# Attention products that name 64 of 128 rows: maxima and scores in a four-layer kernel

## The reference

```python
def _L1_xattn_ref(query, key, values, mask, W_out):      # 16 heads of 16 features, 154 keys
    q = query.reshape(N, Q, HEADS, HEAD_DIM)
    k = key.reshape(N, K, HEADS, HEAD_DIM)
    v = values.reshape(N, K, HEADS, HEAD_DIM)
    energy = jnp.einsum('nqhd,nkhd->nhqk', q, k)
    energy = jnp.where(mask == 0, jnp.float32(-1e+20), energy)
    attn = jax.nn.softmax(energy / jnp.sqrt(jnp.float32(EMB)), axis=-1)
    out = jnp.einsum('nhqk,nkhd->nqhd', attn, v).reshape(N, Q, EMB)
    return out @ W_out.T
x = x + _L1_xattn_ref(_layernorm(x, axis=-1), ctx_1024, ctx_1024, mask_Bx1x1xS2_ik0, L1_xattn_W_out)
```

## Time and profile before

| | |
|---|---|
| median of 3 runs | 815.07 us (814.76 to 815.62) |
| span of the profiled execution | 814.1 us |
| TensorE products busy | 690.2 us, 85% of the span |
| VectorE busy | 632.6 us, 78% |
| ScalarE busy | 486.0 us, 60% |
| attention on TensorE | from about 288 to 545 us |

### The profile page before, as it was taken

How to read it: one execution, slowest core, us unless ns; L and a number is a source line. 1 busy time by engine, 2 the same in 40 slices (tenths; PEclk the granted TensorE clock), 3 DMA queues, 4 the chain that set the end, 5 groups by cost and what they waited for, 6 DMA issues and landing times.

```text
span 814.1 us, 11786 instructions
## 1 busy us (share of the span) xinstructions
PE 690.2 (85%) x4152; PEld 529.5 (65%) x4152; DVE 632.6 (78%) x1244; ACT 486.0 (60%) x621; POOL 313.7 (39%) x249
## 2 busy tenths in 40 slices
PE   6882029999999888999999999999999999009998
PEld 5761026899888754566566656577887888007998
DVE  5988894887777388887767675987888899997654
ACT  2223012554454437796896886666655999796873
POOL 4353604377677735234422420003440444693000
PEclk9995558999999999999999999999999999658999
DMA  9927523456644570010013000003310743201343
GB/s 299 339 81 257 200 80 110 127 137 146 178 88 58 108 254 1 1 47 27 1 47 130 1 27 27 27 27 133 127 52 1 261 152 131 76 0 53 125 135 104
DMA packets 59540, 84.95 MB, mean 104 GB/s; under 512 B 7904, under 2 KB 47712, under 8 KB 57952
## 3 DMA queue, kind: packets, MB, share of 16 engines
q1 hardware_dynamic: 49936, 61.09, 22.3%
q0 software_dynamic: 7872, 21.11, 10.5%
q10 hardware_dynamic: 1680, 2.08, 0.8%
HBM read 53.73 MB, written 30.54 MB: 104 GB/s over the span
## 4 chain that ended last, share of the span: by engine, by line
PE 63%; DVE 14%; ACT 7%; issue 4%; POOL 3%; DMA 1%; POOLq 0%; DVEq 0%; ACTq 0%
PE bank L2101 13%; PE bank L2363 11%; PE bank L2157 8%; PE bank L2387 5%; PE bank L1448 3%; PE bank L1482 3%; PE bank L1505 3%; PE bank L1542 3%; PE bank L1502 3%; DVE above L783 2%; PE bank L1463 2%; PE bank L1486 2%; ACT wgateT L2050 1%; DVE qx L1179 1%; ACT qT L1331 1%
## 5 line engine op out<-in xcount | busy, mean ns | idle before, releaser
L1305 ACT ACTIVATE x<-bank,bic 128x512 f32<-128x512 f32 x160 | 106.2, 697 | 34.1 <-PE bank L1482 32.6
L1179 DVE TENSOR_REDUCE qx<-bank 128x4 fp32r<-128x616 f32 x128 | 98.2, 796 | 27.0 <-PE bank L1448 25.6
L2101 PE MATMUL bank<-ux,uwh 128*128 128x512 f32 x384 | 96.6, 393 | 0.2 <-ACT ux L1995 0.2
L2101 PEld LDWEIGHTS bank<-ux,uwh 128*128 128x128 f32 x384 | 72.5, 189 | 16.0 <-issue 0.6
L1482 PE MATMUL bank<-qT,K 128*128 128x512 f32 x128 | 61.5, 490 | 3.5 <-ACT x L1305 2.0
L2324 ACT ACTIVATE wgateT<-bank 128x512 f32<-128x512 f32 x32 | 19.2, 599 | 65.7 <-PE bank L2363 65.7
L1448 PE MATMUL bank<-Kb,qTb 128*128 128x308 bf16 x256 | 53.2, 298 | 4.9 <-DVE qx L1179 2.2
L2101 PE MATMUL bank<-ux,uwl 128*128 128x512 f32 x192 | 52.0, 393 | 0.0
L1106 POOL CAST qx<-q 128x1024 fp32r<-128x1024 f32 x8 | 8.5, 1068 | 112.7 <-PE bank L1463 104.0
L2363 PE MATMUL bank<-xh,wh 128*128 128x512 f32 x128 | 50.0, 390 | 0.3 <-DVE xl L2297 0.3
L2363 PE MATMUL bank<-xl,wh 128*128 128x512 f32 x128 | 50.0, 390 | 0.0
(11 more groups left out here) (420 smaller groups left out, 2029.0 us busy)
## 6 DMA issues: line engine op xcount, KB each, us to landing
xs_dram<-ux POOLq DMA_DIRECT2D x6, 1024.0 KB, 4.2
ux<-xs_dram POOLq DMA_DIRECT2D x6, 1024.0 KB, 5.3
x_dram<-x SPq DMA_DIRECT2D x4, 1024.0 KB, 5.5
xr<-in_w1T SPq DMA_DIRECT2D x8, 512.0 KB, 3.8
xr<-in_w3T SPq DMA_DIRECT2D x8, 512.0 KB, 4.7
xr<-in_w2T SPq DMA_DIRECT2D x8, 512.0 KB, 6.5
row_dram<-xn SPq DMA_DIRECT2D x8, 512.0 KB, 3.1
x_dram<-xr SPq DMA_DIRECT2D x8, 512.0 KB, 2.9
```

The source lines that it names most:

```text
L1179: dve.tensor_reduce(qx[:, k, g * GH:(g + 1) * GH, MROW].rearrange("p (u h) -> p u h", u=2), pair[i][:].rearrange("p (u x) -> p u x", u=2)[ ...
L1305: act.activation(pr[g % 2][h], S_[u % 2], ACT.Exp, bias=bic[:, s // 2, h // GH:h // GH + 1]).then_inc(p_done, 1)
L2101: mm = pe.matmul(bank[j][:, m * TB:(m + 1) * TB], w[:, c * HI + cols:c * HI + cols + P], x[:, part, c * TB:(c + 1) * TB], start=(w is uwh ...
```

## The change

Both products name the 64 rows that hold something, in the stationary and in the moving operand alike. In `maximum`, u = 0 takes rows 0 to 63 and u = 1 rows 64 to 127. In `score`, heads of even number take rows 0 to 63 and odd ones rows 64 to 127. Nothing else is changed: order, waits, buffers and the work of other engines are the same, and the rows left out were products with zeros.

```diff
                     for u in range(2):
-                        mm = pe.matmul(dst[:, u * QN:u * QN + 2 * S2], qTb[:, k, g, :],
-                                       Kb[s // 2 % 2][:, g, u * 2:u * 2 + 2, :].rearrange("p h s -> p (h s)"), start=True, stop=True)
+                        rows = slice(u * 2 * MW, (u + 1) * 2 * MW)
+                        mm = pe.matmul(dst[:, u * QN:u * QN + 2 * S2], qTb[rows, k, g, :],
+                                       Kb[s // 2 % 2][rows, g, u * 2:u * 2 + 2, :].rearrange("p h s -> p (h s)"), start=True, stop=True)
                     mm.then_inc(sent, 1)
...
                     if h < GH:
                         at = g * GH + h
-                        mm = pe.matmul(dst, K[b % 2][:, at // 2, at % 2, :], qT[s % 2][:, at // 2, :, :].rearrange("p k t -> p (k t)"),
+                        rows = slice(at % 2 * SW, (at % 2 + 1) * SW)
+                        mm = pe.matmul(dst, K[b % 2][rows, at // 2, at % 2, :], qT[s % 2][rows, at // 2, :, :].rearrange("p k t -> p (k t)"),
                                        start=True, stop=True)
```

## The result

The changed kernel takes 830.81 us (828.56 to 831.87, 4 runs) where the kernel before took 814.99 us: +15.8 us, ratio 1.0182 with a 95% interval of 1.0147 to 1.0216. A second series gave 829.37 us and 1.0169 (1.0149 to 1.0189). The forecast was 824.0 us, 810 to 840. The profiled execution of after has a span of 826.8 us against 814.1, +12.7 us, and it is the fastest of the four. Its own time is 828.56 us, 1.8 us above its span, and not 1.0 as I took from the median of before. The runs of the kernel before on record have the same 1.8 us between the two. So its profiled execution was about 0.9 us slower than its median and that of after 2.2 us faster than its own; these two make up the difference between +12.7 and +15.8.

A forecast was written before the change was run, and what follows sets the result against it. TensorE was taken to bound attention's middle. Middle +8.0, first stretch 0 and last +2.8 us, less 2 for further waits, gave +9 us: 823 us on the profiled execution, 824.0 as median, range 810 to 840.

The forecast's parts named there:

- What bounds: Attention's middle, 345 to 510 us: TensorE bounds it, its products busy 163.26 of 165.00 us.
- The gain of a pair: Two products of a maximum run at once, saving 0.13 us a pair, at most 16.6 us in all.
- The sign that I named: In the changed kernel, a pair of maxima's piece of the chain would be near 0.13 us.
- The price of a change: Each new switch of row height costs 0.11 us ahead of a maximum, mostly 0.20 us elsewhere; 25 a steady step.
- What hides: Idle time right ahead of changes in the middle cuts their 24 us to 19.3, leaving +8.0 us after the gain.
- the 2 us taken off: Over all steps, waits not right ahead of a change take up another 2 us of the loss.
- The last stretch: Attention's end: 20 changes at 0.20 us make 4.0 us, of which 2.8 us are left after waits.
- The first stretch, put at 0: Attention's start: changes less gain make +2.7 us, taken as 0 because engines wait for each other.
- The clock rival: Half-height products count for less and TensorE's clock falls to 1.2 GHz for a while: 834 us and above, chance 0.04.
- The median: Whole kernel: the median time stands 1.0 us above the profiled span, turning 823 into 824.0 us.

The follow-up runs named there:

- mx_same: Against mx_only, both products of a pair of maxima take rows 0 to 63, so they can't run at once: 835.69 us, ratio 1.0240.
- probe64: Kernel before plus an unused product of 64 rows and 8 columns ahead of each score: 838.89 us; the same with 128 rows as control: 820.92 us.
- mx_only: Changed kernel with the edit in `score` undone, so only the maxima name 64 rows: 823.53 us, ratio 1.0107.
- score_only: Changed kernel with the edit in `maximum` undone, so only the scores name 64 rows: 839.93 us, ratio 1.0297.
- after_again: The changed kernel run once more with no edit, for its first stretch: 829.37 us, ratio 1.0169.
- after_warm: Changed kernel plus one unused product of 128 rows and 512 columns ahead of each maximum of the second step: 828.57 us, ratio 1.0168.
- same_rows: Changed kernel with both products of each maximum on rows 0 to 63, scores still half-height: 833.34 us, ratio 1.0209.
- dummies64: Kernel before with only the unused products at its start and in the first step named over 64 rows: 829.63 us, ratio 1.0155.

## Why the prediction was right, step by step

- **What bounds.** TensorE in the middle: right, 163 of 165 us before and after.
- **The gain of a pair, 0.13 us.** Right in size: mx_same gives 0.10 net of waits. The sign that I named, a piece of the chain of 0.13 us, was wrong: the piece is 0.24 and the score's 0.22, which together are the 0.46 us from the pair's start to the next product, the wait behind the score included. The starts show the concurrency, the pieces of the chain don't.
- **The price of a change, 0.11 and 0.20 us, taken over from columns and one product over one row.** Right in size. probe64 gives 0.08 us for each change ahead of a short product or behind one, mx_only 0.11 and score_only 0.13, all net of waits; the chain shows +0.20 on L1507 and +0.19 on L1488. Most of it falls on the neighbours of the half-height products, as counted.
- **What hides.** The middle was forecast at 8.0 us in 5.7 steps, 1.4 us a step, before the 2 us taken off; measured 1.19 us a step. Right, a little too high.
- **The last stretch.** From 492.9 us the forecast has 2.8 us and 0.8 us for the rest of the middle, 3.6 together; measured 2.28.
- **The first stretch, put at 0.** This term was mis-sized. At the first mark, 377.59, the forecast has 1.6 us (1.13 steps of the middle); measured 5.57. From attention's own start it is 6.30. The clock has a part in it: it was low for a quarter of that stretch in the profile (column 0.88). As an estimate, if all 13.7 us of low clock cost as much as the 6.9 by which after and after_again differ (1.78 us), the clock took some 3.5 us and the changes of the first steps some 2.8. I had counted 2.7 us of changes there and let the waits take all of them. How the 6.30 us really divide isn't settled; after_warm, with the clock at 1.00, has 5.15 of them left, but 16 products more on the way.
- **Luck.** In span the change cost 12.7 us where 9 were forecast, a miss of 3.7 us, and it would have been larger had the parts not missed in opposite ways: the first mark was 4.0 us later than forecast, the four steps behind it were 0.8 us cheaper (4.77 for 5.6) and the rest 1.3 us cheaper (2.28 for 3.6), while the 2 us taken off for waits were not there.
- **The clock rival.** I gave it a chance of 0.04, as an alternative to the forecast, at 834 us and above. It came true beside the forecast, in spells, and only in the first stretch, where TensorE has waits. In the middle, at 163 of 165 us busy, the clock stayed at 1.00.
- **The median.** +15.8 us against +12.7 us in the profiled spans: the profiled execution is the shortest of four (spans of the others 828.7 to 830.1 us). Over the eight runs of the changed kernel on record the clock, as the mean of the whole execution, goes with the span: the lowest (0.921, twice) has 830.1 and 830.7 us, the highest (0.934) 826.2. But 0.928 stands beside both 826.8 and 829.3, so it explains a part only.

## What to carry to other kernels

Naming only the rows that hold something can pay where half-height products stand next to each other; each switch between heights cost 0.08 to 0.13 us here, in the drain and in a weight load that was hidden before. Count the switches in the order of issue first, price one from a place in the trace where the shape changes, and keep zeros in the idle rows where neighbours are full-height: that was the faster form here. Unused products held the clock here when they were full-height and lost it when they were half-height.

## What the runs showed of the hardware

- Two products of 64 rows in different halves and banks run at once, also a bf16 maximum beside a fp32 score (starts 0.01 us apart in same_rows).
- A change of rows between 64 and 128 costs 0.08 us net of waits in probe64 (0.10 at the place shown), with half of a bare bf16 load in it. A change of columns costs about as much: 0.20 us ahead of a score, less the 0.11 of a bare fp32 load, is 0.09. With the change the next weights are not loaded ahead: L1507's load comes 0.46 us behind the score's and not 0.13.
- While 22 half-height products of 512 columns ran with no gap, the clock fell from 1.00 to 0.50, and TensorE stayed at 1.2 GHz though busy 12.00 of 12.00 us (dummies64); with the same products full-height it read 1.00. The Trainium skill, page "TensorE: Matmul & The Clock Gate", section "Part 1: The HAM clock gate (the "warmup" mystery)", says that how busy the PE has been sets the clock; by these rows, being busy isn't the whole of it, and the height of the products counts.
